# A decoder layer on one core: where the row sums of the attention are taken, and in which steps the query scores stand

## The reference, cut to what matters

```python
q = _rotary((_ln(x, qn_w, qn_b) @ q_w + q_b) as (b, 16, 512, 32), x, rh_w, rh_b)
k = _rotary(k, x, rh_w, rh_b)              # k, v from _ln(x, kvn_w, kvn_b) @ kv_w + kv_b
qn, kn = _ln(q, ln_w, ln_b), _ln(k, ln_w, ln_b)
scores = jnp.einsum('bhqd,bhkd->bhqk', qn, kn) / np.sqrt(HD)     # 16 heads, HD = 32
a = jnp.einsum('bhqk,bhkd->bhqd', jax.nn.softmax(scores, axis=-1), v)
x = _layernorm(x + a @ out_w + out_b)
```

## Time and profile before

| | |
|---|---|
| median of 3 runs | 2241.63 us (2241.44 to 2246.32) |
| the profiled execution | 2242.11 us, its span 2240.1 us |
| mean granted TensorE clock | 0.933 |
| TensorE, VectorE, ScalarE, GpSimd busy | 85%, 69%, 42%, 38% |
| the three phases | attention to about 1,198 us of the span, then retention, then coupling |

### The profile page before, as it was taken

The page is one execution under the profiler, slowest core; times in us unless marked ns, Lnnn a source line. Parts: engine busy times, 40 slices in busy tenths (PEclk is TensorE's granted clock), DMA queues, the critical chain, the costliest instruction groups (busy, mean ns, idle before and its releaser), DMA issues. The chain is left out here.

```text
span 2240.1 us, 29863 instructions
## 1 busy us (share of the span) xinstructions
PE 1914.1 (85%) x9560; PEld 1367.4 (61%) x9560; DVE 1547.2 (69%) x3014; ACT 937.3 (42%) x1564; POOL 859.3 (38%) x785
## 2 busy tenths in 40 slices
PE   4589999999899999999884999999967888888872
PEld 4455655656555665655533888888855766667651
DVE  4557778686786867777654666666644687888766
ACT  2044444444444444444342222222214677766753
POOL 1667758577585757758500222222220000000000
PEclk9789999999999999999886999999997999999986
DMA  4122131321322222222314111111122101122111
GB/s 138 28 53 82 46 108 46 93 59 39 105 56 84 56 58 82 56 79 52 87 29 155 38 68 59 61 57 58 54 76 80 45 35 72 57 76 76 57 38 56
DMA packets 90749, 148.73 MB, mean 66 GB/s; under 512 B 16560, under 2 KB 19632, under 8 KB 90672
## 3 DMA queue, kind: packets, MB, share of 16 engines
q1 hardware_dynamic: 90672, 147.76, 21.9%
...
## 5 line engine op out<-in xcount | busy, mean ns | idle before, releaser
L626 ACT ACTIVATE a_probs<-a_exp 128x512 f32<-128x512 f32 x512 | 290.6, 595 | 476.8 <-PE a_exp L735 472.5
L464 DVE TENSOR_REDUCE a_neg_max<-a_max 128x1 f32<-128x512 f32 x512 | 338.2, 687 | 213.0 <-PE a_max L720 209.3
L720 PE MATMUL a_max<-a_stack 96*128 96x512 f32 x512 | 235.0, 477 | 39.4 <-DVE a_neg_max L464 33.0
L311 POOL TENSOR_TENSOR a_rstd<-a_rstd,a_minus_half 128x16 f32<-128x16 f32 x64 | 191.9, 2998 | 71.2 <-DVE a_rstd L449 71.2
L735 PE MATMUL a_exp<-a_stack 100*128 100x512 f32 x512 | 196.6, 426 | 25.0 <-ACT a_probs L626 19.1
L697 PE MATMUL a_t<-a_w_hi,a_zT_hi 128*128 128x384 f32 x512 | 188.4, 368 | 32.5 <-DVE a_v L430 24.5
L720 PEld LDWEIGHTS a_max<-a_stack 96*128 96x128 f32 x512 | 100.0, 196 | 160.7 <-DVE a_neg_max L464 97.7
L698 PE MATMUL a_t<-a_w_lo,a_zT_hi 128*128 128x384 f32 x512 | 183.3, 358 | 0.0
L699 PE MATMUL a_t<-a_w_hi,a_zT_lo 128*128 128x384 f32 x512 | 183.2, 358 | 0.0
L1027 POOL TENSOR_TENSOR r_part<-r_part 128x512 f32<-128x512 f32 x32 | 45.8, 1431 | 314.9 <-DVE r_part L1074 314.9
L1777 PE MATMUL f_l<-f_h_hi,f_w_hi 128*128 128x512 f32 x240 | 105.1, 438 | 49.4 <-DVE f_h_lo L1476 48.5
...
## 6 DMA issues: line engine op xcount, KB each, us to landing
a_stack<-a_nT_hi SPq DMA_DIRECT2D x512, 64.0 KB, 2.0
a_stack<-a_nT_lo SPq DMA_DIRECT2D x256, 64.0 KB, 2.0
...
```

Of the source, the lines that this page charges most:

```text
L311: nc.gpsimd.tensor_tensor(rstd[:, c], rstd[:, c], minus_half[:, :], ALU.pow).then_inc(pool_step, 1)
L464: nc.vector.tensor_reduce(neg_max[:, t, ROW + h:ROW + h + 1], bank_max[i % 2][:, :], AX_X, ALU.max, negate=True).then_inc(max_done, 1)
L626: nc.scalar.activation(probs[:, kt % 2, h, :], bank_exp[i % 2][:, :], ACT.Exp, scale=float(1.0 / np.sqrt(np.float32(HD)))).then_inc(exp_do ...
L720: mm(bank_max[i % 2][:, :], stack[0:ROW, par, h, t * P:(t + 1) * P], stack[0:ROW, par, HG + h, :], start=True, stop=True).then_inc(score_d ...
```

## The change

- The row sums leave TensorE. `sum_exps`, new on ScalarE, takes the exponential of each query score in place in its bank, with the row's negated maximum as bias and the accumulator's output as the row sum: 16 per group, each behind the exponentials of the same step. A third bank holds query scores in place of `bank_sum`; query score i waits for row sum i-3.
- The 16 sums of a query row (128x16) are inverted once (`invert`, VectorE, step 1), copied out to 32 columns each, transposed by TensorE (`spread_inverse`, step 11) and copied by ScalarE (`save_inverse`, step 12). `normalise` is one product of 128x512 at the end of step 15.
- Since both exponentials must use the same argument, 1/sqrt(32) moves into the head weights.
- The steps: query scores stand in steps 1 to 14 (before 2 to 13), the transposes of the maxima in step 15 (before 14). `save_max` copies for two heads one after the other, and VectorE (`spread_max`) for the other two. `attn_hi` and `attn_low` move to step 0.

```diff
-DVE_STEPS, POOL_STEPS = 55, 40
+DVE_STEPS, POOL_STEPS = 31, 40
...
-QS_DONE = tuple(min(max(4 * (i - 1) // 3, 0), T * HG) for i in range(16))
+QS_DONE = tuple(min(8 * i // 7, T * HG) for i in range(16))
...
-MAX_AT, SAVE_MAX_AT = 14, 14
+MAX_AT, SAVE_MAX_AT = 15, 15
...
-NORM_AFTER, ATTN_HIGH_AT, ATTN_LOW_AFTER = (15, 15, 0, 1), 2, 3
+INVERT_AFTER, INVERSE_AT, INVERSE_SAVE_AT, ATTN_HIGH_AT, ATTN_LOW_AFTER = 1, 11, 12, 0, 0
+NB = 3
...
+        sums = sb("sums", [P, T, HG])
+        inverses = sb("inverses", [P, T, GQ])
...
-        bank_max = [ps("max0"), ps("max1")]
+        bank_max = [ps("max0"), ps("max1"), ps("max2")]
         bank_exp = [ps("exp0"), ps("exp1")]
-        bank_o, bank_sum = ps("o"), ps("sum")
+        bank_o = ps("o")
...
+            for a in (head_w, head_b):
+                last = nc.gpsimd.tensor_scalar(a[:, :], a[:, :], float(1.0 / np.sqrt(np.float32(HD))), None, ALU.mult)
...
-            def normalise(W, c):
-
-                at = slice(c * P, (c + 1) * P)
-                if c == 0:
-                    dve.wait_ge(pv_done, T * W + T)
-                nc.vector.reciprocal(inverse[:, at], bank_sum[:, at]).then_inc(dve_step, 1)
+            def spread_max(U, par):
+
+                dve.wait_ge(maxrow_saved, 2 * U + 1)
+                nc.vector.tensor_copy(stack[ROW:ROW + HG, par, 2:HG, :],
+                                      stack[ROW:ROW + HG, par, 0, :].bitcast(F32).unsqueeze(1).broadcast_to((HG, 2, S))
+                                      ).then_inc(maxrow_spread, 1)
+
+            def invert(U):
+
+                dve.wait_ge(summed, T * HG * (U + 1))
+                if counts(U):
+                    dve.wait_ge(inverse_done, U)
+                nc.vector.reciprocal(sums[:, :, :], sums[:, :, :]).then_inc(dve_step, 1)
                 dve.wait_ge(dve_step, steps.next())
-                last = nc.vector.tensor_tensor(bank_o[:, at], bank_o[:, at], inverse[:, at], ALU.mult)
...
+                nc.vector.tensor_copy(inverses[:, :, :].rearrange("p t (h i) -> p t h i", h=HG),
+                                      sums[:, :, :].unsqueeze(3).broadcast_to((P, T, HG, HD))).then_inc(inverted, 1)
+
+            def normalise(W):
+
+                dve.wait_ge(pv_done, T * W + T)
+                dve.wait_ge(inverse_saved, W + 1)
+                nc.vector.tensor_tensor(bank_o[:, :], bank_o[:, :], inverse[:, :], ALU.mult).then_inc(attn_done, 1)
...
+            def sum_exps(U, i):
+
+                h, t = divmod(i, T)
+                act.wait_ge(max_done, T * HG * U + i + 1)
+                if i == 0 and counts(U):
+                    act.wait_ge(inverted, U)
+                nc.scalar.activation(bank_max[i % NB][:, :], bank_max[i % NB][:, :], ACT.Exp,
+                                     bias=neg_max[:, t, ROW + h:ROW + h + 1],
+                                     accum_out=sums[:, t, h:h + 1]).then_inc(summed, 1)
+
+            def save_inverse(U):
+                act.wait_ge(inverse_done, U + 1)
+                if counts(U):
+                    act.wait_ge(attn_done, U)
+                nc.scalar.activation(inverse[:, :], bank_t[0][:, :], ACT.Copy).then_inc(inverse_saved, 1)
+
             def save_max(U, par):
                 act.wait_ge(maxrow_done, U + 1)
-                nc.scalar.activation(stack[ROW:ROW + HG, par, 0:HG, :],
-                                     bank_max[1][ROW:ROW + HG, :].unsqueeze(1).broadcast_to((HG, HG, S)),
-                                     ACT.Copy).then_inc(maxrow_saved, 1)
+                for h in range(2):
+                    nc.scalar.activation(stack[ROW:ROW + HG, par, h, :], bank_max[1][ROW:ROW + HG, :],
+                                         ACT.Copy).then_inc(maxrow_saved, 1)
...
                     for m in within(KS_DONE, i):
                         exps(U, m)
+                    if left >= 1:
+                        for m in within(QS_DONE, i):
+                            sum_exps(U + 1, m)
                     if i == ATTN_HIGH_AT and counts(U):
                         attn_hi(U - 1, (g - 1) % G)
+                    if i == INVERSE_SAVE_AT:
+                        save_inverse(U)
...
-                if i >= 2:
-                    pe.wait_ge(max_done, T * HG * U + i - 1)
-                mm(bank_max[i % 2][:, :], stack[0:ROW, par, h, t * P:(t + 1) * P], stack[0:ROW, par, HG + h, :],
+                if i >= NB:
+                    pe.wait_ge(summed, T * HG * U + i - NB + 1)
+                mm(bank_max[i % NB][:, :], stack[0:ROW, par, h, t * P:(t + 1) * P], stack[0:ROW, par, HG + h, :],
...
             def transpose_max(U):
                 pe.wait_ge(max_done, T * HG * (U + 1))
+                pe.wait_ge(summed, T * HG * U + T * HG - 2)
...
-                for bank, sums in ((bank_o, False), (bank_sum, True)):
-                    for h in range(HG):
-                        at = slice(h * HD, (h + 1) * HD)
-                        last = mm(bank[at, :], ones[:, :] if sums else v[:, g, kt, at], probs[:, kt % 2, h, :],
-                                  start=kt == 0, stop=kt == T - 1, tile_position=(0, h * HD))
+                for h in range(HG):
+                    at = slice(h * HD, (h + 1) * HD)
+                    last = mm(bank_o[at, :], v[:, g, kt, at], probs[:, kt % 2, h, :],
+                              start=kt == 0, stop=kt == T - 1, tile_position=(0, h * HD))
...
+            def spread_inverse(U):
+
+                pe.wait_ge(inverted, U + 1)
+                for t in range(T):
+                    last = nc.tensor.transpose(bank_t[0][:, t * P:(t + 1) * P], inverses[:, t, :], ident[:, :])
+                last.then_inc(inverse_done, 1)
```

More of the change, by code:

```diff
@@ L577, in _ @@
                     head_var(1, i // 6, False)
+            spread_max(0, 0)
             for s in range(2):
@@ L580, in _ @@
             run(dve, unit, steps, DVE_STEPS)
-            for c in range(2, T):
-                normalise(G * B - 1, c)
             attn_low(G * B - 1, G - 1)
@@ L675, in _ @@
             act.wait_ge(split_done, 1)
+            for i in range(T * HG):
+                sum_exps(0, i)
             save_max(0, 0)
```

73 lines of the change are left out of this document (44 added, 29 removed).

## The result

The changed kernel takes **2320.35 us** (median of 4 runs, 2311.5 to 2322.9) against 2241.63 for the kernel before on the same chip (three runs, 2241.4 to 2246.3): a ratio of **1.0338 (1.0312 to 1.0363)**, slower by 3.4%. A fourth run of the kernel before, in a slower state of the chip at 2351.1, is left out. The prediction was 2221, faster, with a range of 2180 to 2271; the time lies 49 us outside. The profiled execution took 2322.9 us, its span is 2321.1, against 2240.1 before: +81.0.

The account below looks back on a forecast made before the run. TensorE was taken to bound a group before the change, ScalarE behind key score 4 after it. Seven batches -9, ends -15 and prologue +3 made -21 against 2242.1 us: 2221 us, range 2180 to 2271.

Parts of the forecast that it names:

- Added on ScalarE, s = 0.68: ScalarE, 16 exponentials with a row sum per group: each costs s, between 0.58 and 0.84 us, taken as 0.68.
- Rival 2: Row sums on ScalarE: the readout costs a whole small activation, s = 0.84, so slower, 2271 us; chance 0.20.
- Removed, "reciprocal and a copy 0.7 together": VectorE, each group: the 128x16 reciprocal and the copy to 128x512 take 0.7 us together, an estimate.
- Where the new chain runs: Group start: row sum 0 waits for the inverses' copy, key score 4 comes at T+10.1, not T+7.7: +2.4 us.
- From there ScalarE is the full engine: 16.0 us: Behind key score 4: ScalarE's work sets the time, 16.0 us; TensorE, with 9 us to step 8, keeps pace.
- Clock, "+1.0 for g=2 and g=3": Behind the stop ahead of key score 4: 3 us of low clock in every group, making 29.0 us.
- Rival 3: TensorE rests in steps 8 to 15 too; a second low-clock stretch costs 1.0 us in 28 groups: 2249; chance 0.08.
- g=0 and g=1: First two groups of a batch: g=0 rises from 42.8 to 45.7 us; g=1 takes 30.9, z's low parts 1.9 late.
- Net -3.1 on TensorE: TensorE, each group: row-sum matmuls worth 3.5 us go, four transposes of 0.36 us come, net -3.1 us.
- rival 1: Whole kernel: TensorE stays the bound, -3.1 us in 32 groups and -5 behind, 2138 us; chance 0.12.
- Ends: Three groups behind the last projections -2, -3.5 and -5 us, then -4.6 behind the last weighing; prologue +3.
- DMA, hidden: Query score 0 waits 1.1 us for the stack's transfers, hidden under the later stop; uncovered, 1.1 us a group.

Follow-up runs that it names:

- e13: Changed kernel with the copy of the inverses written as a reduction that gives the same values: 2289.3 us, ratio 1.021.
- e7: Changed kernel with every second row sum cut from 512 to 32 columns (its divisor is then wrong): 2291.5 us, ratio 1.020.
- e11: Changed kernel with VectorE's inversion behind step 0 in place of step 1, one buffer of sums: 2261.6 us, ratio 1.009.
- e3: Changed kernel with query scores and maxima back at their old steps, one buffer of sums: 2220.1 us, ratio 0.990.
- e1: Changed kernel with two buffers of row sums, so the first row sum no longer waits for the copy of the inverses: 2239.3 us, ratio 0.998.
- e4: Kernel before the change, with three of the four rounds of row-sum matmuls left out (its divisor is then wrong): 2185.5 us, ratio 0.974.
- e5: Changed kernel with two buffers of sums, inversion behind step 5, query scores and maxima at their old steps: 2189.9 us, ratio 0.976.
- e2: Changed kernel with two buffers of sums and the inversion behind step 5 in place of step 1: 2205.5 us, ratio 0.983.
- e9: Changed kernel with 26 useless matmuls in TensorE's stop ahead of key score 4, in groups 1 to 3 of a batch: 2290.2 us, ratio 1.021.

## Why the prediction was wrong

**The direction** fell with the step that has ScalarE as the full engine behind key score 4, and with two terms that were too small, the copy and the clock. The order of the chain and both of its waits were right. In the group above the terms add up: 29.0 us forecast, +1.9 up to key score 4, +3.4 from there to row sum 12, +0.4 at the end, less the 1.0 that I had added for the clock, is 33.7; 33.8 were measured.

- *Added on ScalarE, s = 0.68*: right, 0.66 to 0.68 measured. Rival 2 is out. ScalarE's busy time is 1256, not the 1330 forecast.
- *Removed, "reciprocal and a copy 0.7 together"*: measured 0.25 + 1.22 = 1.5. I priced the copy by its shape and not by what runs beside it: the mean just ahead of it starts GpSimd's centring, and the copy stands behind that. e13 prices the 0.53 us of difference at 31 us of the kernel (29 by the ratios), 16 by their length and the rest by what follows them.
- *Where the new chain runs*: the order and both waits are as written (row sum 0 waits 2.6 us for the copy on average, 79.2 us in 31; TensorE's stop is 2.9 to 3.6 in g=1 to 3 of the five batches and 2.1 in g=0). The place is not: T+12.0 in place of T+10.1. 0.8 of it is the copy, 0.9 the low clock under the projections ahead of key score 0; in the g=2 groups where that clock is full, key score 4 comes 1.3 us sooner.
- *"From there ScalarE is the full engine: 16.0 us"*: this step failed. From key score 4 to the end of the group I had 17.9 us; 21.8 were measured (686.33 to 708.15). The work was sized right: 16.4 us of it stand between key score 4 and the readout of row sum 12 (16.1 to 16.4 in g=1 to 3 of the five batches). But the stretch takes 19.4, since ScalarE is not full in it: for 3.1 us (1.8 to 3.1 in those groups) it stands, for key scores above all, most of it while TensorE runs at 1.2 GHz (its rows below). So it is "keeps pace there", said of TensorE, that was wrong. e7 agrees: 3.2 us less of ScalarE's work give back 0.9.
```profile
689.93 0.60 ACT L658 ACTIVATE a_probs<-a_exp 128x512 f32<-128x512 f32 x1 [0.83 <-PE a_exp L778]
...
692.60 1.08 ACT L658 ACTIVATE a_probs<-a_exp 128x512 f32<-128x512 f32 x2 [1.40 <-PE a_exp L778]
```
- *Clock, "+1.0 for g=2 and g=3"*: the mis-sized term. I took one low stretch of 3 us a group from the earlier trace rows. There were 31 us in a batch, not 12: 3 to 7 us behind the stop ahead of key score 4, 3 to 4 behind the stop for the last maximum, which I had not listed as a stop, and the longest stretch of all, some 10 us in each batch, at the border of g=0 and g=1. There TensorE stands three times in a row, twice for z's low parts. They are 2.42 and 1.60 us, and were 0.57 and 1.09 before, with no low clock. The granted clock is 0.50 from 753 to 759. The forecast had the lateness of this place (+2.6 and 1.9 us) and no clock behind it. Rival 3 named this mechanism and got a chance of 0.08 and a price of 1.0 us; the batch grew by 10.3 us, and half of the added 21.9 us of low clock would be 11. That this is no more than a bound shows in e11, which has 22.6 us of low clock and takes 138 us. The rows of that border, first in the kernel before, then in the changed one:
```profile
697.48 1.25 PE L690 MATMUL a_exp<-a_ident,a_z 128*128 128x128 f32 x8 [0.57 <-DVE a_zT_lo L420]
...
700.26 0.44 PE L697 MATMUL a_t<-a_w_hi,a_zT_hi 128*128 128x384 f32 x1 [1.09 <-DVE a_zT_lo L420]
```
```profile
750.05 1.72 PE L728 MATMUL a_exp<-a_ident,a_z 128*128 128x128 f32 x8 [2.42 <-DVE a_zT_lo L427]
...
753.65 1.09 PE L767 MATMUL a_max<-a_ident,a_neg_max 128*100 128x128 f32 x4 [1.04 <-DVE a_neg_max L472]
...
756.34 0.68 PE L735 MATMUL a_t<-a_w_hi,a_zT_hi 128*128 128x384 f32 x1 [1.60 <-DVE a_zT_lo L427]
```
- *g=0 and g=1*: g=0 was near (45.7 against 46.8), but its steps were not tested one by one; e3 and e1 take 4.3 and 3.4 us off it, which the terms given for it don't say. g=1 was 3.8 off, with 10.3 us of low clock, the most of all, about half of it from the stretch that starts in g=0: its key score 0 comes 5.3 to 5.6 us behind the transposes of the maxima, before 3.3.
- *Net -3.1 on TensorE*: e4 shows that removing matmuls alone pays (59 of 79 us), so rival 1 has its substance, and e5 shows that a version of this change keeps 55 us of it.
- *Ends*: I had -2, -3.5 and -5 for the three groups behind the last projections and -4.6 behind them. The first has 29.4 us as before, the second 26.0 against 26.4, and the third with all that follows -6.0. The first two have stops of 1.0 to 2.9 us and 16 and 17 us of low clock (before 14 and 10), which may have taken the gain; no run tried it. The prologue's +2.0 is near the +3.
- *DMA, hidden*: I had 1.1 us where this cover goes. In e1, e2, e3 and e5 the cover is gone, and no stop over 0.5 us for the stack shows in the five batches. Behind them it does: e2 has five such stops of 1.4 to 1.5 us between 988 and 1112, e5 one of 2.9. So the worry was empty for most of the kernel and not for its end.

What stays open: how the loss divides between idle time and clock. e9 prices the clock behind the stop ahead of key score 4 (30 us), e1 that stop with its clock (81 us); e3 (100 us) moves this stop, the one at the end of a group, and the clock at the border of g=0 and g=1 (its g=0 has 0.4 us of low clock in place of 8.8) together. The last two were not tried by themselves.
